# A GRU recurrence with a routed spline layer on one core: one-product steps regrouped on TensorE, and ScalarE's squared difference moved behind the other set's gates

## The chip, the cores and the metric

One core of a Trainium2 chip. The time is that of one execution on the device in microseconds (us); 2480.27 us is the median of three runs of the kernel before (2479.81 to 2484.01). Lower is better. Engines are called PE (TensorE), DVE (VectorE), ACT (ScalarE), POOL (GpSimd) and SP (SyncE, which issues most DMAs).

## The reference, cut to what matters

`x` is 4 x 1024 x 1024 (batch, time, width). A GRU runs over time with weights `W_ih`, `W_hh` of 1024 x 3072, and its states go through a layer norm, a routing to one of 64 slices of 16 dimensions, and a spline on that slice:

```
def cell(h, x):
    gi = x @ W_ih + b_ih
    gh = h @ W_hh + b_hh
    i_r, i_z, i_n = jnp.split(gi, 3, axis=-1)
    h_r, h_z, h_n = jnp.split(gh, 3, axis=-1)
    r = jax.nn.sigmoid(i_r + h_r)
    z = jax.nn.sigmoid(i_z + h_z)
    n = jnp.tanh(i_n + r * h_n)
    h_new = (1.0 - z) * n + z * h
    return (h_new, h_new)
...
x = x + ffn(scan(cell, cond_2048, x), gamma, beta, bases, slopes, scale)
```

## The kernel before, in words

The sequence of 1024 steps is cut into 16 chunks of 64 steps that run beside each other; every chunk but the first starts from a guess that 44 warm-up steps over the end of the chunk before make good. The chunks are held as two **sets** (set 0 and set 1, called a and b below), each with 32 columns (8 chunks x 4 batches) and the 1024 state values laid out as 4 quarters of 256 on 128 partitions. A product of the state with `W_hh` is 64 matmuls of 128x32 weights (the state) against 512 or 256 columns of `w_hi` or `w_lo` (`pe_products`, L581), each into one of four groups of 32 PSUM partitions. The weights and the state are split into a high and a low float16 part.

The stages in order of time:
1. `input_product`: `x @ W_ih` for all tokens, up to about 890 us. The last block's share is left over.
2. 24 warm-up steps with one product (mode HEADS: `w_hi` with the state's high part). Between them PE also computes the input product left over: 6 column blocks (`cb`), each of 8 pieces (`pe_late`, L616 to L632), a piece being 12 full 128x128 matmuls (L626 to L628) into four PSUM banks. A column block holds 4 steps of both sets, and PE does: product of a, piece 2i, product of b, piece 2i+1 (`heads`, L652). DVE evicts the four banks (`dve_late`, L828, the instruction at L832): two inside set b's eighth step and two after it.
3. 20 warm-up steps with three products (mode KEPT/FULL: high x high, low x high, high x low).
4. The 64 steps of the pass: 44 with three products, and the last 20 (mode DIFFS, tiles `DIFF_TILE` on, 10 tiles of 2 steps) with one product of the *difference* between this pass's state and the warm-up's, on top of stored sums which PE adds with an identity matmul (L599).
5. A tail of routing, spline and stores, from about 2380 us.

Each engine has its own instruction stream, in program order; the order within a tile of two steps is a0, b0, a1, b1 (set and step) on PE, ACT and DVE. For one set of a DIFFS step, the chain is: PE's product (L581); ACT's gates `rz` and `not_z` from PSUM (L703, L704); DVE's `rn` (L841), `n_sum` (L859), `z_old` (L861); ACT's tanh (L712); DVE's L867, L871, L876, the transpose into `hi` (L881), which is the input of the next product, and the new state `h` (L886). ACT's `act_diff` (L729 to L732) waits for that transpose, squares the new `hi` and accumulates the squares, so that the kernel can judge at the end of the pass whether the difference ever grew too large. It stood right behind the same set's step, so ahead of the next gates that ACT computes, and it wrote its squares, which nobody reads, to `rz`. DVE's next transpose of that set waits for it (`diff_seen`, L880).

Other work rides on the tile: ACT has the sign (after a0's tanh, L751), the sum of the token rows (after b0's, L736), the squares (after a1's, L740 and L742) and the normalisation (after b1's, L746), and copies the routing hits after b1's gates (L755). DVE has the routing of the tile before between b0 and a1 (L922 to L934) and the scaling between b1 and the next a0 (L905, L907). POOL turns the routing's result into rows and two indirect loads (L1128 to L1138) and then computes rstd and shift (L1112 to L1116), which ACT's normalisation needs. SP stores each `h` (L1236), loads the stored sums and states two steps ahead (L1225, L1229) and the token rows of the tile (L1249), which wait for the store of b1.

Of the kernel before, what the change touches and what calls it, by code (L numbers as in the profile page):

```python
# [11 lines left out]
ACT = mybir.ActivationFunctionType  # L12
# [4 lines left out]
KB = D // P  # L17
# [6 lines left out]
SETS = 2  # L24
COLS = CHUNKS // SETS * BATCH
QUARTERS = P // COLS
QF = D // QUARTERS
# [9 lines left out]
TILES = LEN // 2  # L37
# [29 lines left out]
TB = BW // P  # L67
# [351 lines left out]
def recurrence(nc, ctx, t, h0, gi_dram, sums_dram, states_dram, hs_dram, x_rows, y_rows, tables, late_w, pe_spline, dve_spline, pool_spline):  # L419
# [45 lines left out]
    rz = sb("rz", [P, SETS, RZ])  # L465
# [73 lines left out]
    def pair_of(p, i):  # L539

        return p * TILES + i + WARM // 2
# [17 lines left out]
    def flat(ap):  # L559
        return ap.rearrange("p j f -> p (j f)")  # L560
# [13 lines left out]
    with nc.Block() as block:  # L574
# [36 lines left out]
        def pe_run(pe, it, u, seeds, mode=FULL, after=(None, None)):  # L611
            for s in pe_step(pe, it, u, seeds, mode):
                if after[s]:
                    after[s]()
# [34 lines left out]
        @block.tensor  # L649
        def _(pe):  # L650
            pe.sem_inc(hit_turned, 1)
            def heads(cb):  # L652
                for i in range(LATE_STEPS):
                    pe_run(pe, cb * 2 + i // 2, i % 2, 1, HEADS,
                           after=tuple((lambda k=i * SETS + s: pe_late(pe, cb, k)) for s in range(SETS)))

            with pe.Fori(0, CBLOCKS) as cb:
                heads(cb)
            with pe.Fori(WARM_HEADS // 2, WARM // 2) as it:
                for u in range(2):  # L660
                    pe_run(pe, it, u, 1)

            def one_pass(p, first):
                seeds = p + 2
                if first:

                    for tb in range(TB):
                        pe.wait_ge(late_free[tb], CBLOCKS + 1)
                with pe.Fori(0, 2) as i:
                    for u in range(2):  # L670
                        pe_run(pe, pair_of(p, i), u, seeds)
                def tile(i, ends=None):
                    pe_run(pe, pair_of(p, i), 0, seeds, after=(ends, None))
                    pe_run(pe, pair_of(p, i), 1, seeds, after=(None, lambda: pe_turn(pe, p * TILES + i - 1)))

                with pe.Fori(2, DIFF_TILE - 2 if first else TILES) as i:
                    tile(i)
                if first:
                    pe.wait_ge(rows_split, 5)
                    tile(DIFF_TILE - 2, lambda: pe_affine(pe, 0, 0))  # L680
                    tile(DIFF_TILE - 1)
                    with pe.Fori(DIFF_TILE, TILES) as i:
                        pe_run(pe, pair_of(0, i), 0, seeds, DIFFS)
                        pe_run(pe, pair_of(0, i), 1, seeds, DIFFS, after=(None, lambda: pe_turn(pe, i - 1)))
                else:
                    pe_affine(pe, p, 0)
                T = p * TILES + TILES
                pe_affine(pe, p, 1)
                pe_turn(pe, T - 1)
                pe.wait_ge(gap_ready, p + 1)  # L690
                nc.tensor.matmul(misc_bank[:, 64:65], t["ones"][:], gap_over[:], start=True, stop=True)\
                  .then_inc(gap_summed, 1)
                pe_turn(pe, T)
                pe_affine(pe, p, 2)

            passes(pe, one_pass)
            pe_spline(pe)
# [30 lines left out]

        def act_diff(act, it, u, s):  # L729
            act.wait_ge(hi_ready[s], steps_to(it, u) + 2)  # L730
            nc.scalar.activation(rz[:, s, 0:QF], flat(hi[:, s]), ACT.Square,  # L731
                                 accum_out=diff_norm2[:, s, bass.ds(from_diffs(it) + (u + 1), 1)]).then_inc(diff_seen[s], 1)  # L732

        def act_sum(act, T):
            act.wait_ge(h_tok_loaded, T * 16)
            nc.scalar.activation(xhat[:], h_tok[:], ACT.Copy, accum_out=row_sum[:]).then_inc(sum_ready, 1)  # L736
# [12 lines left out]
        def act_signs(act, T):  # L749
            act.wait_ge(signed_ready, T)  # L750
            nc.scalar.activation(signs[:], signed[:], ACT.Sign).then_inc(signs_ready, 1)  # L751
# [7 lines left out]
        @block.scalar  # L759
        def _(act):  # L760
            for s in range(SETS):
                act.sem_inc(hi_ready[s], 1)
            with act.Fori(0, CBLOCKS) as cb:
                for i in range(LATE_STEPS):
                    for s in range(SETS):
                        act_step(act, cb * 2 + i // 2, i % 2, s, 0, HEADS)
            for tb in range(TB):
                act.wait_ge(late_free[tb], CBLOCKS + 1)
            for s in range(SETS):
                act_keep(act, WARM_HEADS // 2 - 1, 1, s)  # L770
            with act.Fori(WARM_HEADS // 2, WARM // 2) as it:
                for u in range(2):
                    for s in range(SETS):
                        act_step(act, it, u, s, 0, after_tanh=lambda: act_save(act, it, u, s))
                        act_keep(act, it, u, s)

            def one_pass(p, first):
                turns = p + 1
                if first:
                    act.wait_ge(rows_split, 5)  # L780
                for s in range(SETS):
                    if first and s == 0:

                        act.wait_ge(hi_ready[s], WARM + 1)
                        act.sem_inc(hi_ready[s], 1)
                        continue
                    act.wait_ge(turned[s], steps_to(pair_of(p, -1), 1) + turns)
                    nc.scalar.activation(hi[:, s], h_turned[:, s], ACT.Copy, scale=S_SCALE).then_inc(hi_ready[s], 1)
                for u in range(2):
                    for s in range(SETS):  # L790
                        act_step(act, pair_of(p, 0), u, s, turns)

                def tile(i, modes, routed):
                    it, T = pair_of(p, i), p * TILES + i
                    act_step(act, it, 0, 0, turns, modes[0], after_tanh=(lambda: act_signs(act, T - 1)) if routed else None)
                    if first and modes[0] == DIFFS:
                        act_diff(act, it, 0, 0)
                    act_step(act, it, 0, 1, turns, modes[0], after_tanh=lambda: act_sum(act, T))
                    if first and modes[0] == DIFFS:
                        act_diff(act, it, 0, 1)  # L800
                    act_step(act, it, 1, 0, turns, modes[1], after_tanh=lambda: act_squares(act, T))
                    if first and modes[1] != FULL:
                        act_diff(act, it, 1, 0)
                    act_step(act, it, 1, 1, turns, modes[1], after_gates=(lambda: act_hit(act, T - 1, i - 2)) if routed else None,
                             after_tanh=lambda: act_normalise(act, T, i - 1))
                    if first and modes[1] != FULL:
                        act_diff(act, it, 1, 1)

                tile(1, (FULL, FULL), False)
                with act.Fori(2, DIFF_TILE - 1 if first else TILES) as i:  # L810
                    tile(i, (FULL, FULL), True)
                if first:
                    tile(DIFF_TILE - 1, (FULL, LAST), True)
                    with act.Fori(DIFF_TILE, TILES) as i:
                        tile(i, (DIFFS, DIFFS), True)
                T = p * TILES + TILES
                act_signs(act, T - 1)
                act_sum(act, T)
                act_squares(act, T)
                act_normalise(act, T, TILES - 1)  # L820
                act_hit(act, T - 1, TILES - 2)
                act_signs(act, T)
                act_hit(act, T, TILES - 1)

            passes(act, one_pass)
# [157 lines left out]
        def _(dve):  # L983
# [6 lines left out]
            with dve.Fori(0, CBLOCKS) as cb:  # L990
                for i in range(LATE_STEPS):
                    for s in range(SETS):
                        if i * SETS + s < KB - 1:
                            dve_step(dve, cb * 2 + i // 2, i % 2, s, 1, HEADS)
                        else:

                            dve_step(dve, cb * 2 + i // 2, i % 2, s, 1, HEADS, lambda: dve_late(dve, cb, 0), lambda: dve_late(dve, cb, 1))
                            dve_late(dve, cb, 2)
                            dve_late(dve, cb, 3)
            for s in range(SETS):  # L1000
                dve_low(dve, s, WARM_HEADS + 1)
                dve.sem_inc(lo_ready[s], WARM_HEADS)
# [645 lines left out]
```

## Time and profile before

| | |
|---|---|
| median of 3 runs | 2480.27 us (2479.81 to 2484.01) |
| the profiled execution | 2479.73 us, span in the trace 2478.2 us |
| PE busy | 2335.3 us (94%) |
| DVE busy | 1303.3 us (53%) |
| ACT busy | 661.4 us (27%) |
| POOL busy | 210.6 us (8%) |
| one-product steps with late pieces | 894.25 to 1155.74 us |
| three-product steps | 1155.74 to about 2164 us |
| difference steps | about 2172 to 2379 us |

A row of a timeline gives the start (us from the start of the span), the duration (us), the engine, the line, the operation, what it writes and reads, how many were merged, and in brackets how long the engine was idle before it and what ended the idle time. PE's matmuls are pipelined: the time from one start to the next is their pace, and the duration is longer than that.

### The profile page before, as it was taken

How to read it: one execution, taken by the hardware profiler on the slowest of the kernel's cores; microseconds unless marked ns; L12 is line 12 of the kernel's file. 1: busy time of each engine (PE TensorE's matmuls, PEld its weight loads, DVE VectorE, ACT ScalarE, POOL GpSimd, SP SyncE). 2: the span in 40 equal slices, each digit the busy share in tenths (PEclk: the TensorE clock that was granted, in tenths of full speed). 3: DMA queues.
4: the chain of work that ended last, by engine and by line, in shares of the span. 5: the costliest groups of instructions: out<-in, count | busy, mean ns of one | idle time of the engine just before them, and what ended most of it. 6: DMA issues, size and time to landing. Idle time of an engine off the chain costs nothing. (4 is left out here: it accounts for less than half of the span.)

```text
span 2478.2 us, 83692 instructions
## 1 busy us (share of the span) xinstructions
PE 2335.3 (94%) x35300; PEld 1277.8 (52%) x35300; DVE 1303.3 (53%) x2691; ACT 661.4 (27%) x1333; POOL 210.6 (8%) x440
## 2 busy tenths in 40 slices
PE   7999999999999989999999999999999999967736
PEld 3444444444444445455666656666666666633312
DVE  4322121212122357777666655666666666888877
ACT  3200000000001123333333333333333333355530
POOL 0000000000000000000000000111111111122225
PEclk9999999999999999999999999999999999999965
DMA  7693131313132445444444443444444444477730
GB/s 236 208 332 127 52 127 52 127 52 127 51 144 103 153 150 152 141 138 134 137 135 135 135 134 101 120 119 116 114 119 119 115 116 118 122 215 232 229 93 5
DMA packets 177335, 330.61 MB, mean 133 GB/s; under 512 B 24272, under 2 KB 87168, under 8 KB 176192
## 3 DMA queue, kind: packets, MB, share of 16 engines
q1 hardware_dynamic: 145360, 267.53, 34.4%
q10 hardware_dynamic: 24192, 44.05, 4.8%
q0 software_dynamic: 7680, 17.57, 4.4%
q8 instruction: 75, 1.23, 0.2%
q14 instruction: 28, 0.23, 0.0%
HBM read 222.39 MB, written 156.77 MB: 153 GB/s over the span
## 5 line engine op out<-in xcount | busy, mean ns | idle before, releaser
L581 PE MATMUL banks<-w_hi,hi 128*32 128x512 f16 (+1 forms) x13824 | 605.0, 328 | 55.7 <-DVE hi L881 43.0
L581 PEld LDWEIGHTS banks<-w_hi,hi 128*32 128x32 f16 x13824 | 359.8, 97 | 284.8 <-DVE hi L881 53.7
L314 DVE SCALAR_TENSOR_TENSOR out_stage<-acc,bias_row 128x512 f32<-128x512 f32 x168 | 116.1, 691 | 622.0 <-PE acc L372 622.0
L581 PE MATMUL banks<-w_hi,lo 128*32 128x512 f16 (+1 forms) x8192 | 354.9, 326 | 0.0
L581 PE MATMUL banks<-w_lo,hi 128*32 128x512 f16 (+1 forms) x8192 | 354.9, 326 | 0.0
L370 PE MATMUL acc<-w_hi,x_even 128*128 128x512 f16 x768 | 291.7, 380 | 13.5 <-DVE x_even L306 11.1
L371 PE MATMUL acc<-w_hi,x_even 128*128 128x512 f16 x768 | 291.6, 380 | 0.0
L372 PE MATMUL acc<-w_lo,x_even 128*128 128x512 f16 x768 | 291.6, 380 | 0.0
L581 PEld LDWEIGHTS banks<-w_lo,hi 128*32 128x32 f16 x8192 | 217.8, 97 | 115.0
L581 PEld LDWEIGHTS banks<-w_hi,lo 128*32 128x32 f16 x8192 | 217.8, 97 | 115.0
L707 ACT ACTIVATE rz<-sums 128x512 f32<-128x512 f32 x176 | 110.9, 630 | 534.5 <-DVE sums L846 534.3
L846 DVE SCALAR_TENSOR_TENSOR sums<-banks,stage 128x512 f32<-128x512 f32 x176 | 121.5, 690 | 238.3 <-PE banks L581 238.2
L370 PE MATMUL acc<-w_hi,x_keep 128*128 128x512 f16 x576 | 218.3, 379 | 0.2 <-issue 0.2
L371 PE MATMUL acc<-w_hi,x_keep 128*128 128x512 f16 x576 | 218.3, 379 | 0.0
L372 PE MATMUL acc<-w_lo,x_keep 128*128 128x512 f16 x576 | 218.3, 379 | 0.0
L712 ACT ACTIVATE n_act<-n_sum 128x256 f32<-128x256 f32 x216 | 90.2, 418 | 178.7 <-DVE n_sum L859 178.7
L370 PEld LDWEIGHTS acc<-w_hi,x_even 128*128 128x128 f16 x768 | 75.3, 98 | 104.7 <-issue 11.7
L372 PEld LDWEIGHTS acc<-w_lo,x_even 128*128 128x128 f16 x768 | 75.2, 98 | 91.0 <-issue 0.8
L371 PEld LDWEIGHTS acc<-w_hi,x_even 128*128 128x128 f16 x768 | 75.3, 98 | 90.6 <-issue 0.6
L717 ACT ACTIVATE hi<-h_turned 128x256 f16<-128x256 f32 x174 | 72.5, 417 | 158.9 <-DVE h_turned L890 158.9
L871 DVE TENSOR_TENSOR n_sum<-not_z,n_act 128x256 f32<-128x256 f32 x216 | 92.6, 429 | 36.8 <-ACT n_act L712 36.8
L886 DVE TENSOR_TENSOR h<-n_sum,z_old 128x256 f32<-128x256 f32 x216 | 90.3, 418 | 20.4 <-DVE n_sum L871 7.4
(172 smaller groups left out, 2162.8 us busy)
## 6 DMA issues: line engine op xcount, KB each, us to landing
stage<-gi_scratch SPq DMA_DIRECT2D x704, 96.0 KB
gi_scratch<-out_stage ACTq DMA_DIRECT2D x168, 256.0 KB, 2.0
stage<-sums_scratch SPq DMA_DIRECT2D x40, 512.0 KB
stage<-in_xT SPq DMA_DIRECT2D x32, 512.0 KB, 6.6
y<-in_x_rows SPq DMA_DIRECT2D x32, 512.0 KB, 4.3
hs_scratch<-h SPq DMA_DIRECT2D x128, 128.0 KB
x_keep<-hs_scratch SPq DMA_DIRECT2D x32, 512.0 KB, 3.9
y<-hs_scratch POOLq DMA_DIRECT2D x32, 512.0 KB
```

The lines of the kernel that those rows point to most:

```text
L314: nc.vector.scalar_tensor_tensor(out=out_stage[:, tb], in0=acc[e % BANKS][:], scalar=UNSCALE, in1=bias_row[:].rearrange("p q f -> p (q f)" ...
L370: nc.tensor.matmul(acc[e % BANKS][:], hi, wh, start=k == 0, stop=False)
L371: nc.tensor.matmul(acc[e % BANKS][:], lo, wh, start=False, stop=False)
L372: last = nc.tensor.matmul(acc[e % BANKS][:], hi, wl, start=False, stop=k == KB - 1)
L581: last = nc.tensor.matmul(bank[q * COLS:(q + 1) * COLS, 0:b - a], state[:, s, j], w[:, j, q * QW + a:q * QW + b], start=first and j == 0, ...
L707: nc.scalar.activation(rz[:, s], sums[:, s, 0:RZ], ACT.Sigmoid).then_inc(rz_ready[s], 1)
L712: nc.scalar.activation(n_act[:, s], n_sum[:, s], ACT.Tanh).then_inc(n_ready[s], 1)
L717: nc.scalar.activation(hi[:, s], h_turned[:, s], ACT.Copy, scale=S_SCALE).then_inc(hi_ready[s], 1)
L846: nc.vector.scalar_tensor_tensor(out=sums[:, s, 0:RZ], in0=rz_bank[s], scalar=UNSCALE, in1=gi[:, s, u, 0:RZ], op0=ALU.mult, op1=ALU.add).t ...
L871: nc.vector.tensor_tensor(new_n[:, s], not_z[:, s], n_act[:, s], ALU.mult).then_inc(new_n_ready[s], 1)
L886: nc.vector.tensor_tensor(h_new, new_n[:, s], z_old[:, s], ALU.add).then_inc(h_ready[s], 1)
```

## The change

PE's one-product steps: the products of a and b follow each other, then the two pieces. DVE evicts all four banks of a column block behind its last step. In the difference steps, ACT squares a set's difference behind the *other* set's next gates, ahead of that set's tanh, and writes the squares to `lo` in place of `rz`; the last one (b1 of the last tile) follows the loop.

```
-                    pe_run(pe, cb * 2 + i // 2, i % 2, 1, HEADS,
-                           after=tuple((lambda k=i * SETS + s: pe_late(pe, cb, k)) for s in range(SETS)))
+                    pe_run(pe, cb * 2 + i // 2, i % 2, 1, HEADS)
+                    for k in range(i * SETS, (i + 1) * SETS):
+                        pe_late(pe, cb, k)
...
-            nc.scalar.activation(rz[:, s, 0:QF], flat(hi[:, s]), ACT.Square,
+            nc.scalar.activation(flat(lo[:, s]), flat(hi[:, s]), ACT.Square,
                                  accum_out=diff_norm2[:, s, bass.ds(from_diffs(it) + (u + 1), 1)]).then_inc(diff_seen[s], 1)
...
-                    act_step(act, it, 0, 0, turns, modes[0], after_tanh=(lambda: act_signs(act, T - 1)) if routed else None)
-                    if first and modes[0] == DIFFS:
-                        act_diff(act, it, 0, 0)
-                    act_step(act, it, 0, 1, turns, modes[0], after_tanh=lambda: act_sum(act, T))
-                    if first and modes[0] == DIFFS:
-                        act_diff(act, it, 0, 1)
-                    act_step(act, it, 1, 0, turns, modes[1], after_tanh=lambda: act_squares(act, T))
-                    if first and modes[1] != FULL:
-                        act_diff(act, it, 1, 0)
-                    act_step(act, it, 1, 1, turns, modes[1], after_gates=(lambda: act_hit(act, T - 1, i - 2)) if routed else None,
-                             after_tanh=lambda: act_normalise(act, T, i - 1))
-                    if first and modes[1] != FULL:
-                        act_diff(act, it, 1, 1)
+                    def gates(u, s, then=None):
+
+                        def after():
+                            if modes[u * s] in (DIFFS, LAST):
+                                act_diff(act, it - 1 if (u, s) == (0, 0) else it, u if s else 1 - u, 1 - s)
+                            if then:
+                                then()
+                        return after
+
+                    act_step(act, it, 0, 0, turns, modes[0], gates(0, 0), (lambda: act_signs(act, T - 1)) if routed else None)
+                    act_step(act, it, 0, 1, turns, modes[0], gates(0, 1), lambda: act_sum(act, T))
+                    act_step(act, it, 1, 0, turns, modes[1], gates(1, 0), lambda: act_squares(act, T))
+                    act_step(act, it, 1, 1, turns, modes[1], gates(1, 1, (lambda: act_hit(act, T - 1, i - 2)) if routed else None),
+                             lambda: act_normalise(act, T, i - 1))
...
                     with act.Fori(DIFF_TILE, TILES) as i:
                         tile(i, (DIFFS, DIFFS), True)
+                    act_diff(act, pair_of(p, TILES - 1), 1, 1)
...
                     for s in range(SETS):
-                        if i * SETS + s < KB - 1:
-                            dve_step(dve, cb * 2 + i // 2, i % 2, s, 1, HEADS)
-                        else:
-
-                            dve_step(dve, cb * 2 + i // 2, i % 2, s, 1, HEADS, lambda: dve_late(dve, cb, 0), lambda: dve_late(dve, cb, 1))
-                            dve_late(dve, cb, 2)
-                            dve_late(dve, cb, 3)
+                        dve_step(dve, cb * 2 + i // 2, i % 2, s, 1, HEADS)
+                for tb in range(TB):
+                    dve_late(dve, cb, tb)
```

## Rows read from the trace of the kernel before

**Rows 1.** Busy time by engine in stretches: one-product steps, part of the difference steps

```profile
894.25:1155.74 261.49, 261.49 (x3648) 130.61 (x3648) 181.48 (x402) 91.64 (x196) 0.00 (x0) 0.99 0.47 138
2200.00:2300.00 100.00, 71.82 (x1361) 38.91 (x1353) 83.75 (x205) 56.02 (x138) 28.57 (x60) 1.00 0.80 231
```

(The columns: the stretch, its length, then busy us of PE, PEld, DVE, ACT and POOL with their instructions, PE clock, DMA share, GB/s.)

**Rows 2.** Timeline of PE in the one-product steps

```profile
1029.92 0.38 PE L626 MATMUL banks<-late_ring,x_keep 128*128 128x512 f16 x1
...
1031.00 0.38 PE L628 MATMUL banks<-late_ring,x_keep 128*128 128x512 f16 x1
1031.31 2.78 PE L581 MATMUL banks<-w_hi,hi 128*32 128x512 f16 x64
1034.03 0.39 PE L626 MATMUL banks<-late_ring,x_keep 128*128 128x512 f16 x1
```

**Rows 3.** Timeline of PE where the three-product steps begin

```profile
1155.74 2.78 PE L581 MATMUL banks<-w_hi,hi 128*32 128x512 f16 x64
1158.35 2.77 PE L581 MATMUL banks<-w_lo,hi 128*32 128x512 f16 x64
```

**Rows 4.** Timeline of all engines over one set's one-product step

```profile
1004.26 2.78 PE L581 MATMUL banks<-w_hi,hi 128*32 128x512 f16 x64
...
1006.32 0.69 DVE L846 SCALAR_TENSOR_TENSOR sums<-banks,stage 128x512 f32<-128x512 f32 x1 [1.23 <-PE banks L581]
...
1010.14 0.45 DVE L890 STREAM_TRANSPOSE h_turned<-h 128x256 f32<-128x256 f32 x1
1010.62 0.42 ACT L717 ACTIVATE hi<-h_turned 128x256 f16<-128x256 f32 x1 [1.57 <-DVE h_turned L890]
```

**Rows 5.** Line L841 (rn), what its idle time waited for (us, times)

```profile
  ACT rz L703: 18.3, 20
```

**Rows 6.** Timeline of DVE over a1 and b1 of a difference tile, and the next tile's L905

```profile
2206.51 0.42 DVE L841 SCALAR_TENSOR_TENSOR rn<-banks,rz 128x256 f32<-128x256 f32 x1
...
2209.63 0.38 DVE L886 TENSOR_TENSOR h<-n_sum,z_old 128x256 f32<-128x256 f32 x1
2210.92 0.43 DVE L841 SCALAR_TENSOR_TENSOR rn<-banks,rz 128x256 f32<-128x256 f32 x1 [0.91 <-ACT rz L703]
...
2213.86 0.38 DVE L886 TENSOR_TENSOR h<-n_sum,z_old 128x256 f32<-128x256 f32 x1
2214.16 1.21 DVE L905 TENSOR_TENSOR x_keep<-x_keep,gamma_s 128x1024 f32<-128x1024 f32 x1
...
2234.74 1.22 DVE L905 TENSOR_TENSOR x_keep<-x_keep,gamma_s 128x1024 f32<-128x1024 f32 x1
```

**Rows 7.** Timeline of ACT over the same tile, from b0's sum on

```profile
2203.06 1.06 ACT L736 ACTIVATE x_keep<-x_keep 128x1024 f32<-128x1024 f32 x1 [1.10 <-DMA x_keep<-hs_scratch]
...
2209.02 0.19 ACT L742 ACTIVATION_READ_ACCUMULATOR x_keep<-x_keep,neg_mean 128x1 f32 x1
2209.83 0.42 ACT L731 ACTIVATE rz<-hi 128x256 f32<-128x256 f16 x1 [0.62 <-DVE hi L881]
...
2210.24 0.58 ACT L703 ACTIVATE rz<-banks 128x512 f32<-128x512 f32 x1
...
2212.37 1.24 ACT L746 ACTIVATE x_keep<-x_keep,shift,rstd 128x1024 f32<-128x1024 f32 x1
```

**Rows 8.** Timeline of PE: the product of b1 in that tile

```profile
2203.69 2.78 PE L581 MATMUL banks<-w_hi,hi 128*32 128x512 f16 x64 [0.69 <-DVE hi L881]
```

**Rows 9.** Timeline of POOL in that tile

```profile
2212.03 0.19 POOL L1116 TENSOR_TENSOR shift<-neg_mean,rstd 128x1 f32 x1 [0.17 <-POOL rstd L1114]
```

**Rows 10.** Timelines of ACT and DVE in the one tile with a late shift

```profile
2357.54 1.24 ACT L746 ACTIVATE x_keep<-x_keep,shift,rstd 128x1024 f32<-128x1024 f32 x1 [1.39 <-POOL shift L1116]
...
2358.81 1.23 DVE L905 TENSOR_TENSOR x_keep<-x_keep,gamma_s 128x1024 f32<-128x1024 f32 x1 [0.69 <-ACT x_keep L746]
```

**Rows 11.** Timeline of SP's queue: b1's state stored, token rows loaded

```profile
2214.49 0.58 SPq L1236 DMA_DIRECT2D hs_scratch<-h  x1
...
2219.54 0.39 SPq L1249 DMA_DIRECT2D x_keep<-hs_scratch  x1
```

## The prediction

> **What bounds the kernel now.** I read the busy time by stretches first. In the one-product steps PE is busy for all of the 261.49 us, DVE for 181.48 and ACT for 91.64 [rows 1]: only PE's own work counts there. In 100 us of the difference steps no engine is full: DVE 83.75, PE 71.82, ACT 56.02, DMA share 0.80 [rows 1]. That is a chain, and the question is which waits lie on it. The timelines answer for each stretch.
>
> One-product steps, PE. A product starts at 1031.31 and the next piece at 1034.03, 2.72 us later [rows 2]. The same 64 matmuls followed by others of their kind take 1158.35 - 1155.74 = 2.61 us [rows 3]. So going from a product to a piece costs 0.11 us. Inside a piece the matmuls start (1031.00 - 1029.92) / 5 = 0.216 us apart, but from the last of a piece to the product it is 0.31 us [rows 2]: going back costs 0.09 to 0.10 us. Both together are 0.21 us for each set and step, and PE pays them 48 times.
>
> Difference steps, DVE. From b1's L841 on, its step and the scaling L905 behind it follow each other without a gap to speak of: 2210.92 to 2213.86 is the step, and the next instruction starts 0.30 us after the start of L886 [rows 6]. Ahead of b1's L841 there is a gap: L886 starts at 2209.63 and L841 at 2210.92, 1.29 us in place of 0.30, with ACT's gates named [rows 6]. This wait comes 20 times, 18.3 us in all [rows 5], so at b0 and b1 of each of the 10 tiles, where no routing or scaling stands between the two sets' steps. What holds the gates is ACT's program order, not PE: the product of b1 began at 2203.69 [rows 8], and if its first bank takes as long as a one-product step shows (2.06 us from the product to L846, [rows 4]), it was there at 2205.8. ACT is idle from 2209.21, waits 0.62 us for a1's transpose, squares it at 2209.83 and only then computes b1's gates at 2210.24 [rows 7]. Ahead of a0 and a1 DVE has 2.5 us of scaling or routing, which covers the same square.
>
> **Part 1, PE's new order.** For each step of both sets: product, product, piece, piece. That is two changes of kind where there were four, and 24 steps save 0.21 us each: **-5.0 us**. Nothing is added on PE. Bounds: 0 if the 0.21 us belongs to each piece or each product for another reason than the change of kind (the trace has no two pieces in a row), and 24 x 0.25 = 6.0 by the reading error of two or three hundredths at each side. I take 5.0, since a product next to a product is shown to cost nothing extra [rows 3].
>
> On this cost the Trainium skill has a rule (TensorEngine Tiling (Array Packing), section Key Properties): changing the tiling mode drains TensorE. The page gives no time; TensorE: Matmul & The Clock Gate, section Single matmul latency, has a constant of 166 ns for a warm single matmul, and as an estimate from it 48 fewer changes would give 8.0 us where the rows give 5.0. The measured gap decides for the sum.
>
> What covers this? Set b's chain now starts behind a's, because DVE runs them in order. Count from the start of a's product; the new step is 2 x 2.61 + 24 x 0.216 + 0.21 = 10.6 us (10.82 before). a: L846 at +2.06, the transpose at +5.88, `hi` complete at 6.36 + 0.42 = +6.8 [rows 4]; needed at +10.6. b: L846 can follow a's transpose at 5.88 + 0.45 = +6.35, though b's bank is there at +4.7; its chain is as long (4.7 us from L846 to the end of L717 [rows 4]), so `hi` of b is complete at +11.1 and needed at 10.6 + 2.6 = +13.2. Slack 2.1 us. ACT has nothing queued between.
>
> The evictions: four in a row, each of L846's kind and shape (0.69 [rows 4]), behind b's transpose, from +10.7 to +13.4. Queued behind them is the next a's L846, which could start at 10.6 + 2.06 = +12.7; it comes 0.8 us late, six times, and eats slack of 3.8 (a) and 2.1 (b). PE wants the banks free at 10.6 + 5.2 = +15.8, 2.4 us after. The first evictions wait for the last piece, whose four banks complete one after the other up to about +10.8, no later than DVE comes to them. SP's loads of the pieces still go out as soon as a slot is used, and each has two steps, 21 us, until its use. All this costs nothing. If the cover went, b's chain would set the period.
>
> **Part 2, the squares.** An instruction pair (0.42 for the square [rows 7], 0.19 as the accumulator's read [rows 7]) leaves the place between tanh and gates and comes between gates and tanh of the other set, 40 times; the number of instructions is the same. Writing float16 to `lo` costs what float32 did: L717, with float16 out and the same shape, takes 0.42 too [rows 4]. `lo` is read by nobody in these steps.
>
> At b0: the gates no longer wait, and L841 follows L886 after 0.30 us: 1.29 - 0.30 = 0.99 us, ten times, **-9.9 us**. Behind the gates ACT now waits for a0's transpose, and queued behind that wait is b0's tanh; but DVE makes that transpose before it begins b0's step, so the square (0.6 us) is over before `n_sum` (two DVE instructions of 0.43 each, as L841 [rows 6], after the gap of 0.30). No loss.
>
> At b1: are the gates ready in time? They can start when the squares of the token rows end, at 2209.02 + 0.19 less the overlap of 0.1, so about 2209.1, and last 0.58: 2209.7, and DVE wants them at 2209.63 + 0.30 = 2209.93. Yes, by 0.2 us. So b1's step also comes 0.99 us earlier, **but what is late next is L905**. It needs ACT's normalisation, which ends at 2212.37 + 1.24 = 2213.61 [rows 7], and that one started 0.15 us after the end of POOL's shift at 2212.22 [rows 9]. POOL's chain starts from the routing's end and does not get shorter. In the tile where it was late, L905 started 0.03 us after the normalisation (2357.54 + 1.24 = 2358.78, L905 at 2358.81 [rows 10]). So L905 can move from 2214.16 [rows 6] to 2213.64 only: 0.52 us, nine times, and 0 in the tile that already waited: **-4.7 us**. Both bounds: 0 if POOL gets later by half a microsecond everywhere, 10 x 0.99 if it kept up after all.
>
> Steps of a keep their length; the first gates behind L905 are computed during 2.5 us of scaling. DVE's period of a tile goes from 20.58 (2214.16 to 2234.74 [rows 6]) to about 19.1. The last square, behind the loop, is where it was. The tail moves earlier as a whole.
>
> **Sum.** -5.0 - 9.9 - 4.7 = -19.6 us against the profiled execution of 2479.73: 2460.1. The median of the runs is 0.54 above that execution, so 2460.7.
>
> **Rivals.**
> 1. *POOL keeps up and b1 gains in full.* Then 2460.7 - 5 = 2455.6. Against it: the 0.15 us between shift and normalisation in this tile. Chance 0.07.
> 2. *DMA becomes late.* The share goes from 0.80 to about 0.80 x 20.6 / 19.1 = 0.86. SP sends b1's store at 2214.49 and can send the load of the token rows only at 2219.54 [rows 11], 5 us later, since the store must land; ACT then still waited 1.10 us for the load [rows 7]. After the change b0 comes 0.99 earlier and b1's scaling waits 0.47, so DVE reaches a1 0.5 us earlier against this load; the sum ends at 2203.06 + 1.06 + 0.19 = 2204.3, a1's gates at 2204.9, wanted at 2206.51 [rows 6]: slack of 1.6 falls to 1.1, plus about 0.2 as the square no longer stands before the gates. If a fuller DMA makes store and load together 2 us later, 0.7 us per tile are given back: 2460.7 + 7 = 2467.7. Chance 0.12. By the Trainium skill (DMA: Bandwidth & Descriptors, section Latency and other measured facts) the access latency of HBM rises from 0.2 us on average to 2 us at high load; that rule speaks for this rival, and no row here shows a store on a quieter queue.
> 3. *The gap on PE is not from the change of kind.* Part 1 gives nothing: 2465.7. Chance 0.05.
> 4. *b1 gains nothing* (POOL's indirect loads late everywhere, as in the one tile): 2465.4. Chance 0.08.
> 5. *Slower: set b's chain sets the one-product step.* Place: b's `hi`, at +11.1 against +13.2. It decides from 2.1 us more on: every microsecond beyond that costs 24 us over the 24 steps, the 19.6 us are used up at 0.8 beyond, and with a chain 4 us longer the time is 2460.7 + 24 x 1.9 = 2506. For it: DVE takes both chains and four evictions in a row. Against: the chain's parts are all in one timeline [rows 4], and nothing joins them. Chance 0.02.
>
> **How the numbers follow.** The forecast case has 0.66. The range takes in rival 1 below and rivals 3, 4 and most of 2 above, so 2455.5 to 2467.5. A measurement of this kernel tells 0.2% from no change, 5.0 us, so faster means below 2475.3: all cases but rival 5 and a heavy form of rival 2. Faster 0.95, same 0.03, slower 0.02.
>
> **What would show it.** Right: products of a and b start 2.61 us apart, pieces follow, one step takes 10.6 us and the stretch 256 us; L841 no longer waits for L703; L905 waits some 0.5 us for L746 in most tiles; difference tiles of 19.1 us. Wrong: PE idle on L717 in the first stretch; a wait of L841 at a1 for gates, behind L736; tiles above 19.5 us or below 18.8.

## The result, and the profile after

The kernel after takes 2473.86 us in the median of 10 runs, against 2480.27 (also ten runs on record): a ratio of 0.9969, with a 95% interval of 0.9961 to 0.9977. The forecast was 2460.7, in a range of 2455.5 to 2467.5. So the change is faster, as forecast, but by 6.4 us in the medians instead of 19.6, and the time lies outside the range. (One of the ten executions took 3372.69 us at a mean granted clock of 0.69; the ratio is taken from the other nine, which lie between 2468.58 and 2477.3 with a median of 2473.68.) The profiled execution took 2474.04 us, 5.7 less than that of before. Lines of the changed part have moved by two to six: L841 is now L847, L881 L887, L886 L892, L905 L911, the square L734, the gates still `rz` (L705).

**The one-product steps went as forecast.** PE's timeline in one of them:

```profile
1035.33 0.38 PE L628 MATMUL banks<-late_ring,x_keep 128*128 128x512 f16 x1
1035.64 5.38 PE L581 MATMUL banks<-w_hi,hi 128*32 128x512 f16 x128
1040.95 0.39 PE L626 MATMUL banks<-late_ring,x_keep 128*128 128x512 f16 x1
```

The two products follow each other. From the start of the first to the next piece it is 5.31 us: 2 x 2.61, and 0.09 to 0.10 for one change of kind, where [rows 2] paid 2.72 for each product. Going back costs 0.31 - 0.22 = 0.09, once per step. The step takes 10.60 us (10.82 before).

**The wait for the gates is gone too.** DVE around b1's step, where [rows 6] had 1.29 us between the two starts and [rows 5] counted 18.3 us:

```profile
2205.39 0.38 DVE L892 TENSOR_TENSOR h<-n_sum,z_old 128x256 f32<-128x256 f32 x1
2205.70 0.41 DVE L847 SCALAR_TENSOR_TENSOR rn<-banks,rz 128x256 f32<-128x256 f32 x1
```

It is 0.31 us here, and the same at b0 and b1 of every tile but one (see the last section). Both edits do what they were meant to do. The difference tiles show where the gain went. DVE's scalings, one per tile:

```profile
2171.03 1.21 DVE L911 TENSOR_TENSOR x_keep<-x_keep,gamma_s 128x1024 f32<-128x1024 f32 x1
2190.34 1.23 DVE L911 TENSOR_TENSOR x_keep<-x_keep,gamma_s 128x1024 f32<-128x1024 f32 x1 [0.68 <-ACT x_keep L749]
...
2249.22 1.22 DVE L911 TENSOR_TENSOR x_keep<-x_keep,gamma_s 128x1024 f32<-128x1024 f32 x1 [0.68 <-ACT x_keep L749]
2271.07 1.23 DVE L911 TENSOR_TENSOR x_keep<-x_keep,gamma_s 128x1024 f32<-128x1024 f32 x1 [0.68 <-ACT x_keep L749]
...
2354.23 1.22 DVE L911 TENSOR_TENSOR x_keep<-x_keep,gamma_s 128x1024 f32<-128x1024 f32 x1 [5.45 <-ACT x_keep L749]
```

The ten periods are 19.31, 19.35, 20.03, 19.50, 21.85, 19.36, 20.10, 19.36, 24.34 and 19.31 us. Five of them are the tile that the change makes possible, 19.3, and a sixth nearly; the other four are longer for one of two reasons. The waits of this stage, 2165 to 2370 us (who waited, for what, then us in all, times, longest):

```profile
ACT x_keep L739 <- DMA x_keep<-hs_scratch: 25.0, 9, 3.6
PE banks L599 <- DMA stage<-sums_scratch: 22.4, 14, 3.1
...
POOL late_out L1140 <- issue: 12.6, 20, 5.3
DVE x_keep L911 <- ACT x_keep L749: 10.9, 9, 5.4
```

And the same of before:

```profile
POOL late_out L1138 <- issue: 7.7, 18, 1.2
...
ACT x_keep L736 <- DMA x_keep<-hs_scratch: 7.5, 10, 1.1
...
PE banks L599 <- DMA stage<-sums_scratch: 3.7, 6, 1.2
```

ACT's wait for the token rows has grown by 17.5 us, PE's for the loaded sums by 18.7. The transfers come later than before. In the trace of before no DMA stands in the chain of waits of these tiles; the page of after gives them a share of the whole span:

```profile
PE banks L581 26%; DMA hs_scratch<-h 2%; DMA x_keep<-hs_scratch 1%; POOL y L1532 1%; DVE n_sum L877 1%; DVE sums L882 0%; DVE banks L1513 0%; DVE z_old L867 0%; DVE late_out L928 0%; PE banks L1438 0%; DVE h L892 0%; POOL late_out L1140 0%; DVE rn L847 0%; DVE x_keep L911 0%; DVE n_sum L865 0%
```

**First reason: b1's store and the load of the token rows are on the chain**, in 5 of the tiles. They get there by two ways. The pieces of the chain in the tile of 21.85 us (start, us, what):

```profile
2248.23 0.32 DVE h L892
...
2248.78 8.49 DMA hs_scratch<-h
...
2257.63 4.26 DMA x_keep<-hs_scratch
...
2263.07 0.49 ACT rz L705
...
2263.65 0.43 DVE rn L847
```

It goes from b1's state through the store (8.49), the load (4.26), ACT's sum over the rows and the gates queued behind it to a1's L847: this is rival 2, at its own place. From one b1's store to the next one's it is 2270.63 - 2248.78 = 21.85 us, the tile's length to the hundredth. In the tiles of 20.03 and 20.10 us the chain takes another way. That of 20.03:

```profile
2209.25 7.10 DMA hs_scratch<-h
...
2216.71 3.83 DMA x_keep<-hs_scratch
...
2221.40 0.36 POOL y L1125
...
2227.17 0.68 POOL rstd L1116
...
2228.45 1.25 ACT x_keep L749
```

POOL's add to y (L1125) waits for the same token rows, and in program order it stands ahead of the row numbers, both indirect loads and the shift. Before, it was out in good time, and the next instruction still waited for DVE's routing:

```profile
2206.80 0.18 POOL L1128 TENSOR_TENSOR row_f<-tile_id,token_row 128x1 f32<-128x1 f32 x1 [1.87 <-DVE late_out L934]
```

Now nothing is left of that slack in this tile: the add goes out at 2221.40, the row numbers follow at 2222.11 without a wait, and shift, normalisation and scaling are 0.7 us late. a1's L847 waits for its gates there too, 0.63 us, but the scaling would have hidden that, since it waits 0.68 us for the normalisation in any case.

From the start of the store to that of the load it was 5.05 us in [rows 11] and is 8.85 in the worst tile. Over the stage, by the starts in SP's timeline, it is 4.4 in the first tile of both kernels; in the nine behind it, 5.9 to 8.85 and 7.0 in the mean, against 4.5 to 5.8 and 4.9 before.

**Second reason: POOL, once, 5 us.** POOL's timeline in the tile of 24.34 us, with ACT's normalisation:

```profile
2341.15 1.01 POOL L1125 DMA_DIRECT2D y<-hs_scratch  x1 [9.82 <-DMA x_keep<-hs_scratch]
...
2343.93 1.21 POOL L1140 DMA_INDIRECT late_out<-hs_scratch,row_now  x1 [0.45 <-issue]
...
2350.47 0.96 POOL L1140 DMA_INDIRECT late_out<-in_x_rows,row_now  x1 [5.33 <-issue]
...
2352.62 0.19 POOL L1118 TENSOR_TENSOR shift<-neg_mean,rstd 128x1 f32 x1 [0.17 <-POOL rstd L1116]
2352.96 1.24 ACT L749 ACTIVATE x_keep<-x_keep,shift,rstd 128x1024 f32<-128x1024 f32 x1 [6.16 <-POOL shift L1118]
```

The second indirect load was not issued for 5.33 us, and the shift that ACT and DVE want is queued behind it. It is the tile of [rows 10], where the same wait was 1.20 us. The trace has the landing of the add that went out at 2341.15 (KB, us to landing):

```profile
y<-hs_scratch POOLq DMA_DIRECT2D x1, 512.0 KB, 8.9
```

So the add landed at 2350.0, and the load went out 0.4 us later. It is the same wherever the landing was recorded, always in the ninth difference tile: e2 (landed at 2354.4, issued at 2354.82), e3 (2342.4, 2342.86) and e6 (2354.6, 2354.99).

**The books**, after less before, in the two profiled executions: one-product steps -4.2; difference tiles from the first scaling to the last 202.51 against 206.31, so -3.8; the start +0.7, the three-product steps +1.5, the tail +0.2. The sum is -5.7 (-5.6 by the rounded terms). In the tiles, ten at 19.32 would be 193.2: the late transfers and POOL's wait cost 202.5 - 193.2 = 9.3 us, 5.0 of them in the one tile.

### The profile page after: what moved, and what is told of

Its sections match the earlier page's. It is cut to its first block and busy times, and to the rows that moved or that the text cites. A ratio compares the mean times of both kernels' runs of the same rounds, so it can differ in the third digit from the quotient of the medians.

```text
span 2472.5 us, 83702 instructions
## 1 busy us (share of the span) xinstructions
PE 2342.8 (95%) x35300; PEld 1287.7 (52%) x35300; DVE 1299.0 (53%) x2691; ACT 658.0 (27%) x1333; POOL 214.4 (9%) x440
## 3 DMA queue, kind: packets, MB, share of 16 engines
q8 instruction: 75, 1.23, 0.2%
## 5 line engine op out<-in xcount | busy, mean ns | idle before, releaser
L581 PE MATMUL banks<-w_hi,hi 128*32 128x512 f16 (+1 forms) x13824 | 613.1, 332 | 30.8 <-DVE hi L887 18.3
L581 PEld LDWEIGHTS banks<-w_hi,hi 128*32 128x32 f16 x13824 | 366.2, 98 | 256.9 <-issue 32.3
L892 DVE TENSOR_TENSOR h<-n_sum,z_old 128x256 f32<-128x256 f32 x216 | 90.2, 417 | 20.4 <-DVE n_sum L877 7.4
```

The lines of the kernel that those rows point to most:

```text
L581: last = nc.tensor.matmul(bank[q * COLS:(q + 1) * COLS, 0:b - a], state[:, s, j], w[:, j, q * QW + a:q * QW + b], start=first and j == 0, ...
L892: nc.vector.tensor_tensor(h_new, new_n[:, s], z_old[:, s], ALU.add).then_inc(h_ready[s], 1)
```

## The experiments

Two theories stood after the result. **D**: transfers are late, because a shorter tile moves the same bytes, and so the chain through DRAM is what ends last; moving transfers away brings the gain back. **P**: POOL's order is at fault (the shift behind two indirect loads), and moving its arithmetic ahead brings the gain back.

**e1 and e2: each part alone.** e1 has the diff's edit to `heads` and to DVE's evictions only, e2 its edit to `act_diff` and ACT's `tile` only.

> Only the new order of PE's one-product steps and DVE's evictions; ScalarE's squares as before. If the two parts add up and the rest of the loss lies in the difference steps: a step of both sets takes 10.60 us, the stretch from the first product to the first three-product step is 4.2 us shorter (24 x 0.21 less 0.9 us for the first pair, whose second product now falls into the stretch of half clock), the difference steps are unchanged at 20.55 us a tile, and the time is 2476 us, with as little scatter as before (under 1 us). If instead the three-product steps pay something for the new order (the changed kernel lost 1.5 us there), 2477.5 or more.

> Only ScalarE's squares moved; PE's order as before. Difference steps alone brought 3.8 us in the changed kernel's trace where 14.6 were forecast. Both theories (a late POOL chain with one long wait in an indirect load's issue; late DMAs) expect 2476 to 2478 us, scatter of several us between executions, and L847's wait for the gates at b0 and b1 gone. A time of 2470 or less would say that the two parts disturb each other.

e1: 2476.24 us against 2480.85 on the same chip, ratio 0.9981 [0.9972, 0.9990]; difference tiles of 20.55 us as before. e2: 2478.88, 0.9989 [0.9979, 0.9998]. So -4.6 and -2.0, together near the -6.4 of both: the parts add up, part 1 is worth nearly what it was said to be, and most of the loss is in part 2. In e2 the same two things happen without part 1: six tiles with store and load on the chain, and one scaling that waits 6.11 us for the normalisation. Two expectations were missed by a little: e2 is 0.9 us above its 2476 to 2478, and e1's stretch of one-product steps was 5.5 us shorter in its profile, not 4.2, since its first step took 12.16 us (13.49 in after).

**e3: theory D, by moving one transfer.** In each tile SP copies 512 KB of rows of x to y, to which POOL later adds. The copies that fall into the difference tiles are sent in tiles 1 to 11 instead; the rest is as in after.

```
...
+                            if ahead == "done":
+                                sp.sem_inc(y_begun, 16)
+                            else:
+                                begin_y(sp, i)
+                            if ahead == "more":
+                                sp.dma_start(whole(y_rows, i + (DIFF_TILE - 2)), whole(x_rows, i + (DIFF_TILE - 2))).then_inc(y_early, 16)
...
```

> The changed kernel, with the copies of x into y of the last 11 tiles (512 KB each) sent during the early three-product tiles, so that the difference steps move some 0.5 MB per tile less each way. Theory D (late DMAs cost the gain: state stores land late, so token rows, sums and gates are late): the 25 us of waits for token rows fall to under 10, the time to 2465 to 2468 us. Theory P (POOL's chain behind the routing sets the scaling, and one indirect load waits 5 us in its issue): less than 2 us better, 2472 to 2474, the scaling still waits 0.7 us for the normalisation in each tile.

2464.51 us (2462.79 to 2469.02), 0.9935 [0.9922, 0.9949]: 9.3 us below after. Of the 7.8 us between the two profiled executions, 5.5 lie in the ten tiles and 2.1 ahead of them, where this edit only adds transfers. The start of that stage differs by about as much between single executions (2171.03 in after, 2169.51 in e7, with the same work ahead of it), so 5.5 is the safer figure for what the copies cost. The waits of the stage:

```profile
ACT x_keep L740 <- DMA x_keep<-hs_scratch: 16.9, 9, 2.5
PE banks L600 <- DMA stage<-sums_scratch: 16.8, 12, 2.3
...
POOL late_out L1141 <- issue: 11.7, 20, 4.4
DVE x_keep L912 <- ACT x_keep L750: 10.7, 10, 4.5
```

The waits for the token rows sum to 16.9 us, not under 10 as theory D expected, but the longest falls from 3.6 to 2.5 us, and that is enough: no DMA is left in this stage's chain, and all tiles are 19.30 to 19.35 us but the one with POOL's wait (4.39 us before its indirect load, a tile of 23.13). The token rows still come late for ACT, but the sum is over before a1's gates are due. Theory D holds for the first reason and not for the second.

**e6: the same copies moved in the kernel before.**

> The kernel before, with the copies of x into y of the last 11 tiles sent early. There the chain through ScalarE's squares sets the tile at 20.55 us and loads were late without being waited for. The theory of late DMAs expects no gain: 2480 us, within 1 us of the kernel before, tiles still 20.55 us, GB/s down to about 205. A gain of more than 3 us would say that the early copies pay by themselves.

2480.67 us against 2480.79, 0.9999 [0.9990, 1.0008]. The stage moves 204 GB/s in place of 231, and nothing gets faster:

```profile
2200.00:2300.00 100.00, 71.66 (x1361) 38.89 (x1361) 83.61 (x205) 56.67 (x138) 27.71 (x60) 1.00 0.74 204
```

So before the change the transfers were hidden, as the forecast had it; what e3 gains is only what the change had put on the chain. (The copies cost nothing in the earlier tiles either.) With the copies gone the add lands after 6.6 us in the ninth tile, and the second indirect load waits 0.49 us where it had waited 1.20.

**e4: theory P.** POOL computes rstd and shift (`between`) between the two indirect loads.

```
...
-            for now, rows in ((pick_now, hs_dram), (x_now, x_rows)):
-                pool.indirect_dma_start(...
+            gather(pool, pick_now, hs_dram)
+            if between:
+                between()
+            gather(pool, x_now, x_rows)
...
```

> The changed kernel, with POOL computing rstd and shift between the two indirect loads in place of behind them. Theory P: the shift is ready 1.5 us earlier, the 0.7 us wait of the scaling goes, and the 5 us wait in the issue of the second indirect load no longer holds the normalisation: 10 x 0.7 + 4 = 11 us less, 2463 us. Theory D: the tiles are held by loads, so a faster chain only waits longer for them: 2470 us or more, with more wait for token rows than 25 us.

2471.87 us (2467.64 to 2472.39), 0.9962 [0.9949, 0.9976]: 2 us below after, not to be told from it with these intervals. (The profiled execution is its fastest, 2467.64; the other four took 2470.18 or more.) No scaling waits any more and the first tiles take 18.54 us, but then they go back to 19 to 22:

```profile
ACT x_keep L739 <- DMA x_keep<-hs_scratch: 40.9, 10, 6.1
...
PE banks L599 <- DMA stage<-sums_scratch: 34.1, 20, 3.8
...
DVE rn L847 <- ACT rz L705: 13.6, 8, 3.3
```

Where after waited 25.0 us for the token rows, this one waits 40.9, and the store lies on the chain in eight tiles. The faster chain waits longer at the same place: P alone is not what holds the kernel.

**e5: both.** The edits of e3 and e4 together.

> The changed kernel with both edits: the copies of the last 11 tiles of x into y sent early, and POOL's rstd and shift between the two indirect loads. If the difference steps are now held by what the DMA engines can move (231 to 236 GB/s in each trace so far, 0.80 of their time, whatever the chain would allow) and by nothing else, then the faster chain shows only where the load is lighter: tiles of 18.55 us as the first two of the run with POOL's order alone, 4.2 MB a tile at 228 GB/s, no 5 us wait on the scaling, and 2453 us. If the early copies only helped by luck of the phases, 2462 us or more.

2460.07 us (2459.02 to 2461.17), 0.9917 [0.9903, 0.9930]. This is the fastest version that still computes everything, 13.8 us below after and 20.7 below before. It is 7 us slower than expected: tiles of 18.54 us four times, then 19.0 to 19.7 with the store on the chain again (6.22 us for the store and 3.91 for the load in the first of six such tiles), and 30.9 us of waits for the token rows in the ten tiles. So it is not a rate at which the DMA engines stop: at 219 GB/s e3 keeps its 19.3 and e5 doesn't keep its 18.5.

**e7 and e8: the add to y made small.** POOL's other transfer adds the 512 token rows of a tile to y. In the difference tiles it moves 1 row of 512 here (`rows` is 0:1), the rest of the add is left out: e7 is after with that, e8 is e5 with that.

```
-            pool.dma_start(whole(y_rows, tile), whole(hs_dram, tile), accum_op=ALU.add, max_dma_last_dim=4096)\
+            pool.dma_start(whole(y_rows, tile)[rows], whole(hs_dram, tile)[rows], accum_op=ALU.add, max_dma_last_dim=4096)\
```

> The changed kernel, in the difference tiles of which POOL's add of the token rows into y moves 1 of 512 rows (the rest of the add is left out). It takes away the transfer that was 8.9 us in landing. If the 5 us wait in the issue of one indirect load is a wait for that add to land, it goes (under 1 us), and with less traffic the token rows are in time: tiles of 19.3 us throughout, 2460 us. If the wait has another cause it stays at 4 to 5 us, 2465 us.

> The kernel with both edits and also only 1 of 512 rows of the add in the difference tiles. If the run with both edits is no longer held by transfers, this one is the same within 1.5 us (2453 us, tiles 18.55 us). If it is still held, this one is faster by what is left, up to 4 us.

e7: 2461.82 us (2461.38 to 2462.66), 0.9923 [0.9908, 0.9938]. DVE's scalings, and the waits of the stage:

```profile
2188.82 1.23 DVE L911 TENSOR_TENSOR x_keep<-x_keep,gamma_s 128x1024 f32<-128x1024 f32 x1 [0.68 <-ACT x_keep L749]
2208.14 1.23 DVE L911 TENSOR_TENSOR x_keep<-x_keep,gamma_s 128x1024 f32<-128x1024 f32 x1 [0.68 <-ACT x_keep L749]
```

```profile
ACT x_keep L739 <- DMA x_keep<-hs_scratch: 15.6, 10, 1.6
...
POOL late_out L1140 <- issue: 6.6, 20, 0.4
```

These are ten tiles of 19.32 us, and both reasons are gone: in them the token rows are never waited for longer than 1.6 us, and the indirect load that had waited 5.33 us now waits at most 0.4. Above all, this run tells what the forecast's two edits are worth when no late transfer is on the chain: ten tiles in 193.2 us, where 206.3 - 14.6 = 191.7 were forecast. That the medians, 2461.82 and 2460.7, are 1.1 us apart is a little closer than that, and in part luck: the profiled execution, 2462.66, is 2.5 above the 2460.1 forecast for one. e8: 2455.13 us, 0.9897 [0.9882, 0.9912], tiles of 18.57 throughout. It is 4.9 us below e5, and 4.9 us is also what its ten tiles save (185.7 for 190.6): so much of e5 was still waiting for transfers.

The windows of the same 100 us in after, e3, e5 and e7, in this order (columns as in [rows 1]):

```profile
2200.00:2300.00 100.00, 77.32 (x1349) 40.42 (x1345) 85.66 (x211) 55.79 (x140) 31.83 (x60) 0.92 0.81 232
```

```profile
2200.00:2300.00 100.00, 78.91 (x1390) 41.38 (x1381) 88.34 (x221) 58.39 (x146) 33.70 (x65) 0.93 0.80 219
```

```profile
2200.00:2300.00 100.00, 80.55 (x1393) 42.21 (x1397) 89.64 (x222) 60.81 (x150) 34.31 (x66) 0.92 0.81 219
```

```profile
2200.00:2300.00 100.00, 81.85 (x1404) 43.03 (x1393) 88.36 (x221) 57.78 (x145) 30.61 (x65) 0.90 0.70 218
```

The share tells little: e3 at 0.80 keeps its tiles, after at 0.81 and before at 0.80 [rows 1] differ in whether the store is late.

**The runs together:**

| kernel | us | tile, us | ten tiles, us | wait for token rows in them, us (longest) | DMA share |
|---|---|---|---|---|---|
| before | 2480.27 | 20.55, one 21.3 | 206.3 | 7.5 (1.1) | 0.80 |
| after | 2473.86 | 19.3 to 24.3 | 202.5 | 25.0 (3.6) | 0.81 |
| e1, PE's part | 2476.24 | 20.55 | 205.8 | 7.7 (1.3) | 0.80 |
| e2, ACT's part | 2478.88 | 19.3 to 24.9 | 202.6 | 27.3 (4.4) | 0.81 |
| e3, copies early | 2464.51 | 19.3, one 23.1 | 197.0 | 16.9 (2.5) | 0.80 |
| e4, POOL's order | 2471.87 | 18.5 to 22 | 199.7 | 40.9 (6.1) | 0.80 |
| e5, both | 2460.07 | 18.5 to 19.7 | 190.6 | 30.9 (4.0) | 0.81 |
| e6, before with copies early | 2480.67 | 20.6 | 205.8 | 3.5 (0.5) | 0.74 |
| e7, small add | 2461.82 | 19.32 | 193.2 | 15.6 (1.6) | 0.70 |
| e8, e5 and small add | 2455.13 | 18.57 | 185.7 | 15.8 (1.8) | 0.64 |

The first column is the median of the runs; the others are from the profiled execution, the share from 2200 to 2300 us.

## Why the prediction was wrong

**Part 1 was right.** -5.0 forecast, -4.6 in the runs of e1, with the 0.21 us per set and step taken from the gap beside each product. The bounds of 0 and 6.0 were not needed, nor rival 3 (no gain) or rival 5 (b's chain): no wait of PE for `hi` in this stage follows the first steps, and the step is 10.60 us to the hundredth. What is missing to 5.0 in after's profile stands in the first step: the stretch lasts 257.3 us and is 4.2 shorter, not 5.0. PE had been idle for 8.46 us ahead of it, and the granted clock of the first 6.05 us is 0.51, the lower of the two levels (1.2 against 2.4 GHz). That step took 13.49 us in after's profile, 2.9 above the others, and 12.63 before, 1.8 above them; in e1's profile it took 12.16. The 166 ns of the Trainium skill (TensorE: Matmul & The Clock Gate, section Single matmul latency), from which 8.0 us were worked out as an estimate, is not what a change of kind costs here: 0.10 and 0.09 us are.

**Part 2, the gates: right.** -9.9 at b0 and -4.7 at b1 assumed that L847 follows after 0.30 us in both; it does, after 0.31. That L905 then waits for the normalisation, and thus for POOL, was right in kind; its wait was put at 0.47 us and is 0.68. The reason is on POOL:

```profile
2187.34 0.26 POOL L1114 TENSOR_SCALAR var_eps<-square_sum 128x1 f32<-128x1 f32 x1
2187.78 0.67 POOL L1116 TENSOR_TENSOR rstd<-var_eps,neg_half 128x1 f32 x1 [0.18 <-POOL var_eps L1114]
2188.62 0.29 POOL L1118 TENSOR_TENSOR shift<-neg_mean,rstd 128x1 f32 x1 [0.17 <-POOL rstd L1116]
```

Before, the three took 0.19, 0.58 and 0.19 us; now 0.26, 0.67 and 0.29, as far as the trace tells because the steps that moved 0.99 us earlier bring other DVE instructions beside them. "POOL's chain does not get shorter" was right; that it gets longer was not thought of. That DVE is the cause was not tested by itself; but in the tile of 24.34 us, where DVE stood idle meanwhile, the three took 0.19, 0.58 and 0.19 us again. The wait is 0.21 us longer than forecast, and an undisturbed tile lasts 19.32 us where 20.55 - 1.51 = 19.04 was forecast: 2.5 us over nine tiles. For the remaining one, whose shift was late before, the forecast had left 20.3 us and e7 has 19.3, so 1.5 us are missing in all. Rival 1 (POOL keeps up) is thereby out, rival 4 (b1 gains nothing) too.

**The step that failed is the sum's silence on transfers.** It took the landing times of before as fixed and gave them a case of their own, rival 2, at a chance of 0.12 and a price of 7 us. The mechanism was right, and partly its place: the slack of a1's gates against the token rows was worked out as 1.3 us after the change, and a store and load some 2 us later than before give back 0.7 us per tile. Measured: store to load start 7.0 in place of 4.9 us in the mean, and three tiles longer that way, by 0.7, 2.5 and 0.8 us: 4.0 in sum. Only the 2.5 came through a1's gates; the other two came through POOL's add, a way that the forecast did not have. Two things were wrong.

1. *The chance.* The share of 0.80 in [rows 1] was scaled to 0.86 and taken for a mild load. But the share hardly rose: it was 0.81 at 232 GB/s in the same 100 us (0.80 and 231 before), and 0.82 at 239 GB/s from 2190 to 2350 us (0.79 and 230 before). The tile gave way instead. A chain in which store, load and sum have 1.3 us of slack per tile does not need a full DMA to break; it needs a landing time that grows a little, and landing times had shown a spread of 4.4 to 5.8 us already before. A forecast that makes tiles 7% shorter with 1.3 us of slack ought to have given rival 2 far more than 0.12.
2. *The price.* It left out POOL's queue. [Rows 10] were read as "POOL's indirect loads late" in one tile, with nothing lost there beyond a 0 for that tile. Behind that row stood a wait that ends 0.4 us after the add has landed. The add went out 4.6 us ahead of the first indirect load before and only 2.8 ahead of it in after, where it landed after 8.9 us (the trace of before lacks that landing), and the wait grew from 1.20 to 5.33 us: 5.0 us in one tile, which no rival priced.

With both, and 0.2 us of the tile of 19.50, it is 9.3 us. The rest of the 14 between forecast and profile is the longer undisturbed tile (1.5), part 1's first step (0.8), and 2.4 us outside the changed steps: the start (+0.7), the tail (+0.2) and the three-product steps (+1.5), where a stretch at the lower TensorE clock lasted 6.8 us in after's profile and 3.4 in before's.

The rule cited with rival 2 from the Trainium skill (DMA: Bandwidth & Descriptors, section Latency and other measured facts: access latency of HBM from 0.2 us on average to 2 us at high load) pointed the right way. The trace agrees in kind: store to load is 2.1 us longer in the mean with nearly the same share. It can't show that HBM's latency is the cause.

**What stays open.** Whether the store is late because of the bytes in flight or because of the order in which the engines serve the queues: e3 and e7 remove transfers of different queues and both help, which tells neither. POOL's long wait ends with the landing of the add, but why it always falls on the ninth difference tile (in before, after and e1 to e5) and on no other, though the adds of the other tiles land as late, was not measured.

## What to carry to other kernels

When an edit shortens a loop whose transfers stay the same, look for every store whose landing releases a load that an engine waits for, and give its landing time a price, by its spread in the trace of before; the mean DMA share does not tell it, and may not even move. A chain through DRAM with about a microsecond of slack per iteration, as here, can be on the critical path as soon as the loop gets a microsecond shorter. List everything that is queued behind an instruction that waits for such a load, on every engine: here it was ACT's gates, and POOL's whole routing behind an add that no engine waited for in this stage. Transfers that nobody waits for, like the copies of x here, are best sent in an earlier stage that has room: this cost nothing in e6 and brought 9.3 us in e3 (5.5 of them seen in the tiles), but only after the compute chain had become short enough to need it.

## What the runs showed of the hardware

**An indirect load can wait for an earlier large transfer of the same queue.** POOL's second indirect load of a tile waited 5.33 us for its issue in after, 4.39 in e3, 6.00 in e2, and at most 0.4 in e7, whose only difference from after is the size of the add (512 KB, 8.2 us from issue to landing by the page) issued on POOL before it. In the four runs that recorded it (after, e2, e3, e6) the wait ended 0.4 us after the add landed. It happened in one tile of ten, always the ninth; in the others of after the loads go out while the add is still under way (at 2324.36 and 2325.85, for an add that landed at 2330.1).

**POOL's arithmetic on few elements depends on what DVE runs beside it.** One instruction of the same shape, L1147, in two tiles of after (the first starts 0.03 us after the scaling of 2190.34 us, shown above):

```profile
2190.37 1.26 POOL L1147 TENSOR_TENSOR base<-late_out 128x16 f32 x1 [1.46 <-DMA late_out<-in_x_rows,row_now]
...
2252.11 0.22 POOL L1147 TENSOR_TENSOR base<-late_out 128x16 f32 x1 [4.30 <-DMA late_out<-in_x_rows,row_now]
```

Started with the scaling, which lasts 1.23 us, it takes 1.26 and ends just behind it; at 2252.11, with no scaling beside it, it takes 0.22. In the other tiles it takes 0.22 to 0.84, and wherever it starts inside one of the two scalings it ends just behind that one (at 2292.16, for instance, 0.84 us). By the Trainium skill (SBUF — State Buffer, section SBUF: two separate sides) a DVE instruction with two SBUF inputs and a POOL instruction that reads SBUF lock each other out of a shared port for a whole instruction; the trace agrees with that in these rows, and the 0.07 to 0.10 us by which each of the three instructions ahead of the normalisation got longer could be the same in small. That last was not tested by itself.

**PE falls to the lower clock in this stage, and no tile's length shows it in after, e1 and e7.** Before, the granted clock of 2200 to 2300 us was 1.00 [rows 1]; in after it was 0.92, in e7 0.90. One such stretch, in windows of after:

```profile
2249.00:2252.50 3.50, 0.73 (x4) 0.32 (x4) 3.12 (x4) 1.34 (x5) 0.40 (x2) 1.00 1.04 391
2252.50:2255.90 3.40, 3.40 (x33) 1.28 (x36) 2.37 (x7) 1.36 (x2) 0.16 (x1) 0.51 0.46 178
```

PE had waited 3.09 us for the loaded sums, and the product behind it ran at 0.51, the lower of the two levels (1.2 against 2.4 GHz), and took 4.46 us in place of 2.78. DVE waited 1.70 us for it at b0, in this one tile. The late token rows, which a1 waited for behind it, hid that wait; had they been in time, the late sums and the slow product would have cost most of it. Where the clock was lowest, in e7, every tile still took 19.32 us. In e1 it was 0.93 with tiles of 20.55: the lower clock is not where the gain went.
